# First attention and routing fused, the shared expert as 16 groups ahead of 79 routed ones

## The reference

```python
x = x + tanh(g_xattn[0]) * xattn(layernorm(x), ctx)      # 16 heads, 64 context keys per batch
x = x + tanh(g_ffn[0]) * moe(layernorm(x))
# moe: scores = sigmoid(xt @ gate_w.T); top 4 of 16 by scores + gate_b; w = scores / sum * 2.5
#      y = sum over the 4 chosen experts  w * (silu(xt@w1_e) * (xt@w3_e)) @ w2_e
#      y = y + the shared expert, for every token
x = x + tanh(g_xattn[1]) * causal_xattn(layernorm(x), [ctx, x])
x = x + tanh(g_ffn[1]) * ternary_linear(layernorm(x))
```

## Time and profile before

| | |
|---|---|
| median of 3 runs | 1519.49 us (1517.51 to 1522.52) |
| profiled execution | 1521.21 us, of which the span from first to last instruction is 1519.5 us |
| busy over the span | PE 73%, DVE 66%, ACT 42%, POOL 34% |
| granted PE clock | 0.867 of full speed |
| instructions | 24337 |

### The profile page before, as it was taken

The page is one execution under the profiler, slowest core; times in us unless marked ns, Lnnn a source line. Parts: engine busy times, 40 slices in busy tenths (PEclk is TensorE's granted clock), DMA queues, the critical chain, the costliest instruction groups (busy, mean ns, idle before and its releaser), DMA issues. The chain is left out here.

```text
span 1519.5 us, 24337 instructions
## 1 busy us (share of the span) xinstructions
PE 1104.2 (73%) x8143; PEld 563.9 (37%) x8155; DVE 1009.6 (66%) x1838; ACT 635.5 (42%) x1280; POOL 522.1 (34%) x582
## 2 busy tenths in 40 slices
PE   3799995424235888872377569999999999998857
PEld 2355553212113555541144323333333333331646
DVE  4799985454552444442799378888888888870675
ACT  0446553111111222220233217776777767776430
POOL 1242331676773777776000241211211111111110
PEclk7899996666657999997689759999999999996889
DMA  6101100222267988891688721111211121100003
GB/s 195 34 21 42 32 10 11 78 90 84 88 220 184 201 185 190 185 186 15 252 286 256 205 66 39 38 39 49 65 39 39 41 72 40 39 2 1 1 0 111
DMA packets 190213, 141.82 MB, mean 93 GB/s; under 512 B 127368, under 2 KB 162955, under 8 KB 190106
## 3 DMA queue, kind: packets, MB, share of 16 engines
q1 hardware_dynamic: 166922, 96.89, 24.6%
q0 software_dynamic: 14496, 34.65, 6.6%
q10 hardware_dynamic: 8688, 8.85, 1.8%
HBM read 53.20 MB, written 70.02 MB: 81 GB/s over the span
## 5 line engine op out<-in xcount | busy, mean ns | idle before, releaser
L1796 DVE TENSOR_REDUCE small<-ps 128x2 f32<-128x960 f32 (+6 forms) x384 | 378.9, 1040 | 56.7 <-PE ps L1851 56.4
L1775 ACT ACTIVATE region<-ps 128x512 f32<-128x512 f32 (+5 forms) x768 | 343.1, 532 | 107.7 <-PE ps L1865 106.2
L1746 POOL TENSOR_SCALAR_AFFINE_SELECT region<-region 128x512 f32<-128x512 f32 (+2 forms) x160 | 87.5, 547 | 425.3 <-ACT region L1775 425.2
L1865 PE MATMUL ps<-region 50*128 50x512 f16 (+5 forms) x896 | 197.4, 329 | 27.2 <-ACT region L1775 24.0
L877 POOL DMA_INDIRECT result_rows<-region,small x174 | 176.3, 1014 | 72.4 <-issue 47.8
L1941 PE MATMUL ps<-region 128*32 128x512 f32 (+5 forms) x1792 | 191.5, 501 | 2.5 <-POOL region L1746 1.9
L1213 PE MATMUL ps<-region 128*128 128x384 f16 x696 | 128.8, 337 | 69.3 <-DMA region<-expert_rows 69.1
L870 POOL DMA_INDIRECT expert_rows<-region,small x128 | 130.1, 1017 | 73.1 <-DVE small L1038 36.9
L1851 PE MATMUL ps<-region 48*128 48x480 f16 (+6 forms) x896 | 141.3, 333 | 13.5 <-DVE small L1796 11.3
L1865 PEld LDWEIGHTS ps<-region 50*128 50x128 f16 (+1 forms) x896 | 54.2, 94 | 209.7 <-ACT region L1775 195.3
L1097 DVE SCALAR_TENSOR_TENSOR region<-ps,region 128x384 f32<-128x384 f32 x58 | 32.3, 557 | 137.8 <-ACT region L921 135.8
(11 more groups left out here) (235 smaller groups left out, 1643.9 us busy)
## 6 DMA issues: line engine op xcount, KB each, us to landing
region<-result_rows SPq DMA_DIRECT2D x16, 1024.0 KB, 6.4
region<-v_parts SPq DMA_DIRECT2D x16, 576.0 KB, 4.1
v_parts<-region SPq DMA_DIRECT2D x14, 576.0 KB, 7.0
region<-k_parts SPq DMA_DIRECT2D x96, 68.0 KB, 2.2
region<-q_parts SPq DMA_DIRECT2D x96, 64.0 KB, 2.1
k_parts<-region SPq DMA_DIRECT2D x16, 272.0 KB, 4.2
x_sb<-in_x ACTq DMA_DIRECT2D x8, 512.0 KB, 9.1
region<-in_w13T SPq DMA_DIRECT2D x16, 256.0 KB, 3.0
```

Source lines behind the costliest of these rows:

```text
L1746: nc.gpsimd.affine_select(out=t, in_=t, compare_op=ALU.is_ge, fill=0.0, base=r0, pattern=[[0, G], [1, w]], channel_multiplier=-1).then_inc ...
L1775: nc.scalar.activation(dst, src, ACT.Exp, scale=SCALE).then_inc(s_exp, 1)
L1796: nc.vector.tensor_reduce(nmp[:, qt, :, p0:p0 + np_, place], s_pair(n + first)[:, :, 0:np_ * nk] .rearrange("p e (h k) -> p e h k", h=np_) ...
L1865: ins = nc.tensor.matmul(o, k_of(rr, tbuf)[:, pair, kt * P:kt * P + rows], q_of(rr, tbuf)[:, pair, q0:q0 + nq], start=True, stop=True)
```

## The change

Stages 1 and 2 become one: in the turn of chunk c, the routing of chunk c-1 stands between the steps of the attention on every engine. Both layer norms are applied by ACT (an activation with a scale and a bias for each row) and no longer by DVE; POOL makes the bias by a second small instruction. The gate's matmuls are in float32. The shared expert leaves the routing: the normed rows of each chunk are also stored to `dense_rows` in DRAM, and 16 groups of 256 of them are run through the group pipeline ahead of the routed ones. A group has 256 rows now, with 79 routed ones in the table, two scatters each; y results lie in one PSUM bank. The expert is no longer loaded from a table but is the start shifted right by 13. The weights of the second attention are loaded and split during the groups.

```diff
-GROUP = 3 * P
+GROUP = 2 * P
-STRIDE = B * L + 4 * P
+SHIFT = 13
+STRIDE = 1 << SHIFT
+FIRSTS = B * L // GROUP
+ALL_GROUPS = FIRSTS + GROUPS
-ROW_BUFS = 4
+ROW_BUFS = 2
-Y_BUFS = 5
+Y_BUFS = 6
...
-                for j in range(8):
-                    nc.vector.tensor_copy(maskb[0:1, :, j * CTX:(j + 1) * CTX],
-                                          mneg[0:1, :].rearrange("p (b k) -> p b k", b=B))
+                nc.vector.tensor_copy(maskb[0:1, :, :], mneg[0:1, :].rearrange("p (b k) -> p b k", b=B))
...
+                def rstd_of(layer, c):
+                    n = event[layer, c]
+                    pool.wait_ge(s_var, n + 1)
+                    if n:
+                        pool.wait_ge(s_xn, n * TC)
+                    nc.gpsimd.tensor_tensor(rstd[:], ve[:], half[:], ALU.pow).then_inc(s_pow, 1)
+                    pool.wait_ge(s_pow, n + 1)
+                    nc.gpsimd.tensor_tensor(nmr, nmu, rstd[:], ALU.mult).then_inc(s_rstd, 1)
...
+                for c in range(CHUNKS):
+                    if c:
+                        rstd_of(2, c - 1)
+                    if c >= 2:
+                        send(c - 2, 8, 16)
+                    if c < LAST:
+                        normalise(c + 1, range(2))
+                    if c and c < LAST:
+                        send(c - 1, 0, 2)
+                    if c + 2 < CHUNKS:
+                        rstd_of(1, c + 2)
+                    if c and c < LAST:
+                        send(c - 1, 2, 8)
+                    if c < LAST:
+                        normalise(c + 1, range(2, TC))
...
+                send(LAST - 1, 0, 4)
+                rstd_of(2, LAST)
+                send(LAST - 1, 4, 16)
+                send(LAST, 0, 16)
+                for r in range(GROUPS):
...
+                for c in range(CHUNKS):
+                    if c < LAST:
+                        move_queries(c + 1)
+                    if c:
+                        normalised(2, c - 1)
+                    for expert in experts_beside(c):
+                        high(*expert)
+                    move_probs(c, range(2))
+                    if c:
+                        rows_high(c - 1)
+                        move_rows(c - 1)
...
+                sp.wait_ge(s_tabs, 1)
+                for g in range(G_BUFS, FIRSTS):
+                    if ACT_TAILS + g - G_BUFS < E:
+                        fill_tail(sp, ACT_TAILS + g - G_BUFS)
+                    shared_rows(g)
...
+                for g in range(FIRSTS, ALL_GROUPS):
+                    sp.wait_ge(s_ggu, g - G_BUFS + 1)
+                    first = start(sp, g)
+                    sp.dma_start_transpose(xgT[:, g % G_BUFS].rearrange("p s k n -> p (s k) n"),
+                                           xs[bass.ds(first, GROUP), E:ROW].bitcast(F16)).then_inc(s_xg[g % G_BUFS], 16)
...
+                    sp.dma_start(gidx[:, r % I_BUFS, :],
+                                 xs[bass.ds(first, GROUP), bass.ds(first >> SHIFT, 1)].bitcast(I32)
```

More of the change, by code:

```diff
@@ L773, in flamingo @@
[L773 to L782 removed]
+        fill = view(region1, "fill", [P, ROW], F32)
@@ new lines, in flamingo, with slot, full, moved @@
+            order += rows_of(LAST) + logits_of(LAST) + ranks_of(LAST) + [(LAST, "count", "dve")]
+            turn = {(c, n): i for i, (c, n, _) in enumerate(order)}
+            def slot(c, name):
+                return ps[:, 4 + turn[c, name] % RING, :]
+            def full(c, name):
+                return turn[c, name] + 1
+            def moved(i):
+                return sum(e == order[i][2] for _, _, e in order[:i + 1])
+            norms = [(1, 0), (1, 1)]
+            for c in range(CHUNKS):
+                norms += [(2, c - 1)] if c else []
+                norms += [(1, c + 2)] if c + 2 < CHUNKS else []
@@ L860, in _, with normalise, send @@
+                def normalise(c, tiles):
+                    for j in tiles:
+                        pool.wait_ge(s_rsum, c * TC + j + 1)
+                        pr = probs[c % 2][:, j, :].rearrange("p (h k) -> p h k", k=CTX)
+                        nc.gpsimd.tensor_tensor(pr, pr, rsum[:, j, :].unsqueeze(2).to_broadcast([P, H, CTX]),
+                                                ALU.mult).then_inc(s_prob, 1)
+                def send(c, first, last):
                     b = c % ROW_BUFS
@@ new lines, in _ @@
+                normalise(0, range(TC))
+                for c in range(CHUNKS):
+                    if c:
[12 more added lines that the diff above has]
+                        normalise(c + 1, range(2, TC))
@@ new lines, in _ @@
+                for j in range(TC):
+                    shift(0, j)
+                    if j:
+                        row_sum(0, j - 1)
+                row_sum(0, TC - 1)
+                low(*SHARED)
+                for c in range(CHUNKS):
+                    more = c < LAST
+                    if c:
+                        dve.wait_ge(s_dve, moved(turn[c - 1, "o1"]))
+                        statistics(2, c - 1)
+                    for expert in experts_beside(c):
+                        low(*expert)
+                    if more:
+                        shift(c + 1, 0)
+                    if c:
+                        rows_low(c - 1)
+                    if more:
+                        shift(c + 1, 1)
+                        row_sum(c + 1, 0)
+                    if c:
+                        choose(c - 1)
+                        targets(c - 1)
+                    if more:
+                        shift(c + 1, 2)
+                        row_sum(c + 1, 1)
+                    if c:
+                        slots(c - 1)
+                    if c + 2 < CHUNKS:
+                        statistics(1, c + 2)
+                    if more:
+                        shift(c + 1, 3)
+                        row_sum(c + 1, 2)
+                        row_sum(c + 1, 3)
+                    add(c)
@@ L1095, in group_hidden @@
+                dve.wait_ge(s_dve, moved(turn[LAST, "o1"]))
+                statistics(2, LAST)
+                rows_low(LAST)
+                choose(LAST)
+                targets(LAST)
+                slots(LAST)
+                tables()
                 def group_hidden(g):
```

1028 lines of the change are left out of this document (456 added, 572 removed).

## The result

| | before | after |
|---|---|---|
| median, runs beside each other | 1521.01 us (4 runs, 1517.51 to 1524.66) | 1465.64 us (4 runs, 1464.47 to 1465.75) |
| profiled execution, its span | 1521.21, 1519.5 us | 1465.75, 1464.0 us |
| busy PE, DVE, ACT, POOL | 73, 66, 42, 34% | 77, 69, 45, 34% |

The changed kernel takes 0.963 of the time before, with a 95% interval of 0.961 to 0.966: 55 us less. The forecast was 1446 us: the result lies inside its range, and 20 us above the forecast itself.

The account below looks back on a forecast made before the run. Stage 1 was bound by DVE and PE, stage 2 by a chain of small steps, stage 3 by POOL's scatters and SP. Span 1519.5 - 68.4 (to the last scatter) - 5.5 (stage 4) = 1445.6, median about 1446 us, range 1385 to 1495.

Parts of the forecast that it names:

- N(7): End of POOL's fourth normalise of chunk 7, closing six fused turns; forecast at 344 us.
- the first fetch: First routed group's fetch, after SP's eleven pairs (a tail, a transposing DMA) and one more, 34.8 us; forecast N + 76.5.
- the pace: Time between routed groups' fetches, set by SP: 3.80 less 0.6 (table load) and 0.5 (rows), 2.7 us.
- stage 4: Final combine: first fetch of results issued at the barrier lands 6.4 us later, saving 5.5 us.
- A turn of 43: Fused stage, one chunk: chain of 5.8, 18.5 and 15.2 us, plus 3 for port waits and 0.5 for PE's clock.
- 0.5 for PE at a low clock: Term of the fused turn: 0.5 us for PE running at a low clock after its idle stretch.
- the ring through the queries: Fused turn, absent from the forecast's sum: ACT's norm, PE's transposes, queries, their moves on ACT, then norm, high, low, shift.
- N(1): End of POOL's fourth normalise of chunk 1, start of the six fused turns; forecast at 86.3 us.
- DVE alone: Rival: DVE's own 32 us sets the fused turn, 66 us less, 1380 us; chance 0.14.
- Sends: Rival: POOL's sends slow by 0.75 us each beside a full DVE, turn 49, 1482 us; chance 0.14.
- The issue of a transposing DMA: Rival: in the routed groups this issue doesn't shrink with its rows, pace 3.35, 1497 us; chance 0.15.
- the fixed price: Rival: a routed group costs 3.80 us whatever its rows, 86 us more, 1532 us; chance 0.07.

Follow-up runs that it names:

- e10: e7 with DVE's statistics and add earlier, ACT's norm ahead of the last exponential, three POOL sends behind its power; 1412.5 us.
- e1: Changed kernel with five of POOL's eight sends moved behind the last two normalise; 1468.1 us.
- e2: Changed kernel with all eight of POOL's sends moved behind the last two normalise; 1455.3 us.
- e5: Changed kernel with ACT's two last exponentials of the next chunk ahead of the norm; 1464.8 us.
- e6: Changed kernel with the edits of e2 and e5 together; 1463.0 us.
- e4: Kernel before the change with only the group size altered, to 256 rows and so 79 groups; 1554.2 us.
- e12: e10 with the DVE addition that frees the ranks' PSUM bank moved ahead of the shift of tile 3; 1414.7 us.
- e7: Changed kernel with e2's sends, targets' DMA on ACT, exponential 2 and high earlier on ACT, tile 3's shift ahead of the slots; 1422.0 us.
- e8: Changed kernel with ACT's five tails issued between its first groups instead of ahead of them; 1468.3 us.

## Why the prediction was right, and where it missed

**The sign and the size.** Faster, by 55 us where 73 were forecast. The span is 18.4 us over the sum's 1445.6, made up of: N(7) +2.7, from there to the first fetch +6.4, the pace +12.0 (78 x 0.154), last fetch to last scatter 16.5 instead of 14, +2.3 with rounding, and stage 4 -5.0.

**A turn of 43.** Measured 42.4. From the slots to N it is 14.9 (forecast 15.2). From the first shift to the slots it is 20.2 in the turn at 186 us (18.5 and up to 3 of port waits; they cost 2.1: 0.41 at L901 and 1.73 at L943). From N to the first shift it is 6.4 to 7.3 (5.8). A norm activation takes 0.52 there and not L512's 0.41, a term that was mis-sized. And ACT's norm waits for the queries' moves, which the sum does not have at all, and not for POOL's product alone. PE's transposes and scores do "fit in it", as the text said (the first scores end at 184.1, the first shift starts at 186.4), but the queries ahead of them do not. The "0.5 for PE at a low clock" was too small as well: the queries alone take 1.6 to 3.0 us more than the 3.67 of e10, though in the chain that the sum left out.

The size was right. The mechanism was half of it: taking the sends away does not shorten the turn by what they take, since the ring through the queries is as long (e1, e2, e5, e6). That the missing ring did not move the result is luck: it closed in the same microsecond as the one that was counted. N(1) came at 92.2 and not at 86.3; the slightly shorter turns made up for 3.5 of these 5.9. The head came 0.4 earlier and not 1.5, and from the second tile's `normalise` (80.44) to N(1) it is 11.8, where it was 7.9 before. In e5, with the exponentials ahead of the norm, it is 9.6, so ACT's order holds 2.2 of the 3.9.

**Signs.** POOL did go from the sends straight to two `normalise`, and DVE did wait for ACT ahead of `low`. PE idle ahead of its transposes was wrong, as shown above, and the first scatter came at 442 and not near 434.

**Rivals.** DVE alone does not bound the changed kernel, but its 32 us is what e10 runs into, with 31.4 of busy time. Sends hardly slowed down: their mean was 1.02, and the longest of a turn stood beside L883 (1.96) or L849 (1.34). The issue of a transposing DMA did shrink, to 1.26, and the fixed price is out. The prediction's reading that this issue "hardly varies with the load" was wrong by its own row, whose longest is 2.58; in the changed kernel that of a shared group goes up to 2.31.

**First fetch.** SP's first tail came at N + 43.5 (41.7 for the counts that it waits for), and from there to the fetch it is 39.3 and not 34.8: the step that failed is "eleven pairs of a tail and a transposing DMA of up to 1.49". The pairs beside ACT's tails are longer, and a wait for the shared groups on PE, 2.4 us in one, stands in a path in which the forecast had them hidden.

**The pace.** 2.85, the upper end of the forecast's own span. The sum took off 0.6 for a load (e4: 0.52) and 0.5 for rows (e4: 0.43). Both terms were right within 0.1 and both erred the same way. The 0.5 was to come from the DMA's own issue, which gave 0.24 of it.

**Stage 4.** From the barrier to `combine` it is 4.99 where it was 12.73: 7.7 saved, not 5.5. The first fetch lands 4.8 us after its issue and not 6.4; the 6.4 that I took is the median of sixteen, whose shortest was 4.8 before as well, and the median now is 6.8. The barrier itself comes 4.7 us after the last scatter (6.2), and what follows `combine` is 1.3 shorter.

## What to carry to other kernels

When a sum over one chain comes out near the time, look for the second chain before moving anything: the slack of each operand of the waiting instruction (here 2.9 us at the row sum) bounds what the first edit can be worth. At ACT's norm the two that it waits for are 0.2 us apart, and e1 gained nothing. In a ring over four engines with written orders, an edit pays only with the ones that shorten the other ring; e1, e5 and e12 gave nothing alone or last, and together with moves of statistics, shift, add and `high` the turn fell from 42.4 to 36.3. When an order is changed, look at the granted clock of the matmuls in the ring as well: the same eight took 3.67 us or 5.2 to 6.7, which is more than the edits of e10 and e12 moved. For small groups count what the issuing engine does for each: one 1 KB DMA handed to another engine was worth 17.5 us.

## What the runs showed of the hardware

DVE and POOL hold each other up at short instructions. L943, two inputs of 128 x 256 in SBUF, took 2.15 us whenever it started together with a `normalise` of 1.90, and 0.43 in e7, where it did not. The Trainium skill (SBUF — State Buffer, Who interferes with whom) says that such an instruction and a GpSimd one that reads SBUF exclude each other and the later waits in full; the trace agrees, 0.42 + 1.73. What I had not looked for is a one-input instruction held up too: L843, a `tensor_scalar` of 128 x 4, took 2.20 us instead of 0.17 beside `normalise`. The same section names `tensor_scalar` among those that can take both ports. The rows of the two, first the changed kernel and then e7 (shortest, median, longest ns):

```profile
L843 DVE TENSOR_SCALAR small<-mv x12: 169/170/2206, 92.9 to 341.1; 128x4 f32<-128x4 f32 x12
L943 DVE TENSOR_TENSOR small<-small x7: 426/2148/2151, 119.0 to 364.6; 128x256 f32<-128x256 f32 x7
```

```profile
L948 DVE TENSOR_TENSOR small<-small x8: 425/426/426, 120.8 to 359.0; 128x256 f32<-128x256 f32 x8
```

The issue of a DMA is not of fixed length. A tail's took SP 0.57 to 0.62 us; five or eight issues in a row on ACT took 8.20 and 10.97 us, loads of their row numbers included in the first, while the DMA engines stood at a share of 1.0 and more. A transposing DMA of 256 rows took from 1.25 to 2.31 in the same stretch of the changed kernel, and up to 4.11 in e8.
